# Cross-attention coefficients and a gelu table load later in the loop body, one more wait for GpSimd's subtract, and 60 transposes of the identity before the first expert block

## What is computed

```python
x = x + attn(layernorm(x))            # one head, q = W x/|x|, scores q (A q)^T / 16, softmax, times v, times |x|
x = x + xattn(layernorm(x), context)  # 4 heads of 64, mask, softmax over 1601 rows, @ Wo
# feed-forward
idx = argmax(softmax(x @ Wg + bg))
h   = gelu(x @ W1[idx] + b1[idx])     # 1024 wide
x   = x + h @ W2[idx] + b2[idx]
```

## Time and profile before

| | |
|---|---|
| median of 3 runs | 874.06 us (873.71 to 874.42) |
| the profiled execution's own time | 875.33 us |
| its span, first to last instruction | 873.6 us |
| mean granted TensorE clock | 0.945 of full speed |
| TensorE busy in matmuls | 767.2 us, 88% of the span |
| VectorE busy | 665.9 us, 76% |
| ScalarE busy | 461.4 us, 53% |
| GpSimd busy | 165.2 us, 19% |

### The profile page before, as it was taken

How to read it: one execution, slowest core, us unless ns; L and a number is a source line. 1 busy time by engine, 2 the same in 40 slices (tenths; PEclk the granted TensorE clock), 3 DMA queues, 4 the chain that set the end, 5 groups by cost and what they waited for, 6 DMA issues and landing times. The chain is left out here.

```text
span 873.6 us, 19805 instructions
## 1 busy us (share of the span) xinstructions
PE 767.2 (88%) x6136; PEld 692.5 (79%) x6137; DVE 665.9 (76%) x1608; ACT 461.4 (53%) x930; POOL 165.2 (19%) x254
## 2 busy tenths in 40 slices
PE   3879799989999898999989899998988753999996
PEld 2769689978888797988879788887987642889996
DVE  5974647888887888888888888888888744777773
ACT  2544536665565755656565565666656530444342
POOL 3100121130312303021130302203021111222221
PEclk9999989999999999999999999999999965999999
DMA  6242251321212132131322202132149292011110
GB/s 205 68 134 68 70 197 41 117 85 48 100 36 94 57 104 100 30 100 36 100 75 80 100 30 100 36 124 100 30 133 406 88 357 65 22 39 50 36 32 15
DMA packets 51142, 80.88 MB, mean 93 GB/s; under 512 B 4894, under 2 KB 29216, under 8 KB 50976
## 3 DMA queue, kind: packets, MB, share of 16 engines
q1 hardware_dynamic: 49232, 75.63, 25.9%
q0 software_dynamic: 1872, 4.76, 1.5%
HBM read 45.60 MB, written 35.18 MB: 92 GB/s over the span
## 5 line engine op out<-in xcount | busy, mean ns | idle before, releaser
L1126 ACT ACTIVATE ps_cross<-flip 128x512 f16<-128x512 f32 (+1 forms) x256 | 124.6, 514 | 113.5 <-PE flip L845 92.3
L1351 DVE TENSOR_TENSOR ps_cross<-flip,ps_cross 128x512 f16<-128x512 f32 (+1 forms) x256 | 143.6, 582 | 10.3 <-ACT ps_cross L1126 9.9
L845 PE MATMUL flip<-ident,exp_cross 128*128 128x128 f32 (+1 forms) x832 | 132.3, 282 | 8.5 <-DVE ps_cross L1351 5.1
L834 PE MATMUL scores<-keys_cross,qt 128*128 128x402 f32 x512 | 133.3, 385 | 4.3 <-DVE xneg L1511 2.3
L1312 ACT ACTIVATE exp_cross<-exp_cross,xneg 128x1024 f32<-128x1024 f32 (+1 forms) x128 | 122.7, 960 | 15.1 <-DVE xneg L1511 15.0
L856 PE MATMUL cross_out<-vals_cross,ps_cross 128*128 128x128 f16 (+1 forms) x832 | 105.3, 228 | 28.3 <-DVE ps_cross L1351 28.2
L856 PEld LDWEIGHTS cross_out<-vals_cross,ps_cross 128*128 128x128 f16 (+1 forms) x832 | 78.5, 104 | 51.9 <-DVE ps_cross L1351 36.5
L845 PEld LDWEIGHTS flip<-ident,exp_cross 128*128 128x128 f32 (+1 forms) x832 | 96.0, 143 | 16.3 <-DVE ps_cross L1351 6.6
L722 PE MATMUL scores<-keys_self,u_tile 128*128 128x512 f32 x384 | 102.5, 404 | 6.3 <-issue 4.6
L821 PE MATMUL flip<-vals_self,ps_self 128*128 128x256 f32 x768 | 104.0, 289 | 0.0
L858 PE MATMUL cross_out<-vals_cross,ps_cross 128*128 128x64 f16 (+1 forms) x832 | 98.2, 198 | 0.0
(11 more groups left out here) (197 smaller groups left out, 1240.8 us busy)
## 6 DMA issues: line engine op xcount, KB each, us to landing
rows_dram<-pads SPq DMA_DIRECT2D x17, 520.0 KB, 3.9
w_piece<-W SPq DMA_DIRECT2D x32, 256.0 KB, 2.9
w_dram<-w_high SPq DMA_DIRECT2D x32, 256.0 KB, 2.3
w_dram<-w_piece SPq DMA_DIRECT2D x32, 256.0 KB, 2.7
w1s<-w_dram SPq DMA_DIRECT2D x8, 1024.0 KB, 11.3
w2s<-w_dram SPq DMA_DIRECT2D x8, 1024.0 KB, 10.8
u_dram<-u_out SPq DMA_DIRECT2D x4, 1024.0 KB, 5.9
u_tile<-u_dram SPq DMA_DIRECT2D x16, 256.0 KB, 2.8
```

What stands on the lines that cost most here:

```text
L834: mm = pe.matmul(scores[:, n, 0:KB], qt[:, h, :], keys_cross[:, part, h, n * KB:(n + 1) * KB], start=(part == 0), stop=(part == 1))
L845: tr = pe.transpose(flip[0:rows, bank(use), n * P:(n + 1) * P], exp_cross[:, h % 2, m * P:m * P + rows], ident[:, :])
L1126: return act.activation(out, in_, ACT.Copy, **kw)
L1351: return dve.tensor_tensor(out, full, hi, ALU.subtract)
```

## The change

Four edits. GpSimd's subtract in body j waits for `self_max` of that body too. The three coefficient operations on VectorE move from behind `sneg` to behind `self_lo(1)`, ahead of `cross_max(0,1)`. The one-element gelu moves in body 17 from the front to behind `cross_hi(3,3)`. And TensorE gets 60 transposes of the identity, without a wait, between the last `rank` and the wait for `x2_ready`; they write into a bank of `scores` that nobody reads.

```diff
@@ gpsimd
                 pool.wait_ge(piece_hi, j + 1)
+                pool.wait_ge(self_max, j + 1)
                 pool.tensor_tensor(w_piece[:, :, :], w_piece[:, :, :].bitcast(F32), w_high[:, :, :].bitcast(F32),
                                    ALU.subtract).then_inc(piece_lo, 1)
@@ tensor
         run_pipeline(pe, body)
+
+        for n in range(60):
+            pe.transpose(scores[:, 3, 0:P], ident[:, :], ident[:, :])
         pe.wait_ge(x2_ready, T)
@@ scalar
             a, b, c = k < T, 1 <= k <= T, k >= 2
-            if k == T + 1:
-
-                act.activation(barrier[:, 1:2], ident[:, 0:1], ACT.Gelu).then_inc(gelu_table, 1)
             if c:
                 cross_hi(j, k, 2, 2)
...
             if c:
                 cross_hi(j, k, 3, 3)
+            if k == T + 1:
+
+                act.activation(barrier[:, 1:2], ident[:, 0:1], ACT.Gelu).then_inc(gelu_table, 1)
@@ vector
             if c:
-
-                dve.wait_ge(cross_exp_ready, 8 * (j - 1))
-                dve.tensor_tensor(xcoef[:, 2, :], xden[:, 0, :], xden[:, 1, :], ALU.add).then_inc(o_step, 1)
-                dve.wait_ge(o_step, 3 * (j - 1) - 2)
-                dve.reciprocal(xcoef[:, 0, :], xcoef[:, 2, :]).then_inc(o_step, 1)
-                dve.wait_ge(o_step, 3 * (j - 1) - 1)
-                dve.tensor_scalar(xcoef[:, 1, :], xcoef[:, 0, :], v_scale[:, 1:2], None, ALU.mult).then_inc(o_step, 1)
                 cross_lo(j, k, 3, 0)
                 cross_lo(j, k, 3, 1)
                 cross_lo(j, k, 3, 2)
             if b:
                 cross_max(j, k, 0, 0)
             if a:
                 self_lo(j, k, 0)
             if c:
                 cross_lo(j, k, 3, 3)
             if a:
                 self_lo(j, k, 1)
+            if c:
+                dve.wait_ge(cross_exp_ready, 8 * (j - 1))
+                dve.tensor_tensor(xcoef[:, 2, :], xden[:, 0, :], xden[:, 1, :], ALU.add).then_inc(o_step, 1)
+                ...
+                dve.tensor_scalar(xcoef[:, 1, :], xcoef[:, 0, :], v_scale[:, 1:2], None, ALU.mult).then_inc(o_step, 1)
             if b:
                 cross_max(j, k, 0, 1)
```

More of the change, by code:

```diff
@@ L1558, in body @@
                 self_lo(j, k, 1)
+            if c:
+                dve.wait_ge(cross_exp_ready, 8 * (j - 1))
+                dve.tensor_tensor(xcoef[:, 2, :], xden[:, 0, :], xden[:, 1, :], ALU.add).then_inc(o_step, 1)
+                dve.wait_ge(o_step, 3 * (j - 1) - 2)
+                dve.reciprocal(xcoef[:, 0, :], xcoef[:, 2, :]).then_inc(o_step, 1)
+                dve.wait_ge(o_step, 3 * (j - 1) - 1)
+                dve.tensor_scalar(xcoef[:, 1, :], xcoef[:, 0, :], v_scale[:, 1:2], None, ALU.mult).then_inc(o_step, 1)
             if b:
```

## The result

The changed kernel takes **829.77 us** in the median of 4 runs (826.53 to 830.76), against 873.88 for the kernel before (4 runs beside them, 871.21 to 874.42): a ratio of 0.9495, with a 95% interval of 0.9462 to 0.9527. The forecast was 827.5, with a range of 822 to 836. The profiled execution took 830.19 us, its span 828.4 against 873.6.

The account below looks back on a forecast made before the run. GpSimd's subtract holding VectorE's multiply was taken to pause TensorE and mostly slow its clock. Terms -41.95, -3.8, +0.1, +0.5, +0.3, -1.4, -0.3 sum to -46.55: 828.8 us profiled, 827.5 median, range 822 to 836.

Parts of the forecast that it names:

- The hold: After `sneg`, GpSimd's subtract holds VectorE's 128x4 coefficient multiply for 2.1 us, so `cross_lo(3,0)` is late and TensorE idles 2.08 us.
- A body of 34.1 us: Looped middle bodies fall to 34.1 us (ends 33.3 and 34.7); 12 bodies give -41.95 us (ends -51.5 and -34.8).
- the push: The moved coefficient operations delay `cross_max(0,1)` and `self_lo(2)` on VectorE, charged 0.1 us a body (ends 0 and 0.7).
- The clock: In the loop, TensorE's pause mostly brings the slow clock, worth 1.5 us a body; new bodies should have 1.00.
- Body 15 and 16: Body 15 loses its pause and slow stretch, -3.8 us; in body 16 the coefficients come behind the mask-bias wait, +0.5.
- Body 17: Coefficients stand ahead of the sum over `cross_out`, +0.3 us; the later gelu table load hides in ScalarE's idle time, -1.4.
- GpSimd's wait: The subtract's extra wait on `self_max` costs 0: already met in bodies 3 to 15, hidden in bodies 1 and 2.
- Transposes: 60 transposes behind the last `rank` bring the clock back before the first expert product: -0.3 us (ends -1.75 and +2.7).
- The rival with a chance of 0.32: The 60 transposes stay at the slow clock and hold `flip_x` by 2.7 us: 830.5 us; chance 0.32.
- The rival on the other side: Slower than before: the multiply meets GpSimd's subtract at its new place, TensorE pauses and loses its clock: about 877 us; chance 0.03.
- The sum: All terms over the whole kernel sum to -46.55 us: profiled execution 875.33 to 828.8 us, median 827.5.
- The start: Stretch up to `sneg` of body 3: body 2 gains nothing and pays the push, +0.1 us.

Follow-up runs that it names:

- the meeting at the new place: The changed kernel, but GpSimd's subtract waits for `self_lo(0)`, so it runs while VectorE reaches the moved coefficients: 851.15 us, ratio 0.9748.
- the load alone: The kernel before with only the one-element gelu (the table load) moved behind `cross_hi(3,3)` in body 17: one run, 872.82 us.

## Why the prediction was right, step by step

- **The hold.** Right, and shown: the multiply is at 0.229 us; with the coefficients left in place and the subtract moved behind them the gain is the same or better; with the subtract put back onto them half of the gain goes. The prediction had told apart by rows which operations pass (one input in PSUM) and which do not, and this held for `cross_lo` and `self_lo`. The Trainium skill, "SBUF — State Buffer", section "Who interferes with whom", has a rule of which I made no use: VectorE and GpSimd share a pair of SBUF ports; a VectorE operation with two SBUF inputs contends with a GpSimd operation that reads SBUF, and one in a two-port mode contends with GpSimd, where whoever issues first keeps the pair for the whole instruction. These traces agree: the add (two inputs in SBUF) was held for 1.6 us, the multiply for 2.1, each to the end of the subtract, and no operation with an input in PSUM. That the multiply, with one SBUF tensor and a column of factors, runs in a two-port mode is what the rule would need; no run shows its mode.
- **A body of 34.1 us.** Measured 34.23 in the middle and 34.00 at the end, 410.80 us for 12 against 409.2: the term is 40.35 and not 41.95, the one that was sized wrong by most. I had taken body 13, less its pause, plus 0.1 for the push. In the three kernels without the push (the coefficients at their old place, the subtract behind them) the 12 bodies take 408.82 to 409.47 us. So the push is worth 0.11 to 0.17 us a body, and the rest of the miss is that a body without it takes 34.07 to 34.12 and not 34.01. The prediction kept away from body 2's 33.3 because a looped body pays for its branch and for waits against registers. That such a body is longer is borne out (34.23 against 33.41 after the change, of which 0.44 is idle time of TensorE and 0.38 busy time); what in the loop costs it no run shows.
- **The clock.** Right: 1.00 over all 12 bodies. But the pause alone doesn't decide it: 2.05 to 2.44 us of pause lose it in 11 of the 12 looped bodies before the change and 2.13 us don't in body 13; the 1.65 us of the kernel with the meeting at the new place lose it in none of 12.
- **Body 15 and 16.** Forecast -3.8 and +0.5, so -3.3; measured -3.14 together. Body 16 is a poor place for terms of this size: its wait for the mask bias alone is between under 0.2 and 2.5 us in these kernels.
- **Body 17.** Forecast +0.3 and -1.4; measured -1.6 together. The kernel with the load alone has the same 19.93 us as the changed one, and the one with the coefficients alone 21.62 against the 21.53 before, so the coefficients cost about 0.1 us there and not 0.3: the sum over `cross_out` would wait for its matmuls anyway, and starts 0.14 us behind the last of them where it started 0.04 behind.
- **GpSimd's wait.** Zero was right for this kernel, but the reason was incomplete. I named only ScalarE as the one who might suffer. By itself the wait costs 1.6 us in body 2, since it moves the subtract onto the coefficients; only the other edit made it free.
- **Transposes.** Forecast: the clock back after 3.7 us, the last one 8.4 us behind the first, -0.3 in sum. Measured 3.9, 8.65 and -0.8, with a spread over the kernels that is as large as the effect. The rival with a chance of 0.32, that transposes stay slow, is false: the clock rose in their midst wherever they were tried (no 60 of them took the 12.8 us that slow ones need). Its price was 830.5; the 830.6 in the paragraph on the transposes is 0.1 too high for the same sum. The rule behind it (the Trainium skill, "TensorE: Matmul & The Clock Gate", Part 4) doesn't hold for these fp32 transposes, at 0.213 us each before the rise and 0.109 behind it; what that page measured is a bf16 transpose.
- **The rival on the other side** had the right mechanism and a wrong price. I gave 877 us for a multiply held at the new place, with the slow clock in every body. The run that does it took 851: there it is the add that is held, the pause is 1.65 us and not 2.1, and the clock stays. That GpSimd would not get there by itself was right: it is idle when the coefficients come.
- **The sum.** 828.8 was forecast for the profiled execution, and 830.19 measured. The loop is 1.6 us above its forecast, the start 0.5 and bodies 15 and 16 0.2; body 17 and the transposes are 0.5 each below. That these small terms mostly cancel is luck, and they are within what differs from kernel to kernel without an edit. The 1.27 us between execution and median of the kernel before were 0.42 here, which is the rest of the 2.3 us between 827.5 and 829.77.
- **The start**, +0.6, is for the most part no effect of the change: body 2 has the +0.1 of the forecast (33.41 against 33.30), and the other 0.5 us stand already at the `sneg` of body 1. This one, ahead of which only GpSimd's wait differs, starts between 120.35 and 124.46 us over the twelve kernels.

## What to carry to other kernels

When a tiny operation shows a median far above its minimum, look which other engine's instruction ends at the same moment. Here, where both had all their inputs in SBUF, it was enough to move either. Moving the one that nobody waits for was 1.1 to 2.0 us better over 12 bodies, too little for the times to tell. A wait that orders two engines is only worth what it keeps apart: check each body for what it brings together. And work that is to keep TensorE's clock up must reach up to the work that needs it: 60 transposes with 3.5 to 4.0 us of pauses behind them gave under a microsecond, 87 with pauses of 0.4 and 0.9 us gave 2.2.

## What the runs showed that was not expected

Transposes of fp32 alone, with no other matmul, bring TensorE's clock from 0.50 to 1.00: after 3.9 us in the changed kernel, after 3.2 and 4.4 in the ones with transposes alone and with 70 of them. The clock does not fall at once behind a pause: in the changed kernel it was still 1.00 when the product began behind pauses of 1.58 and 2.04 us, and fell some 1.5 us into it, when TensorE had been busy again. That is not how it always goes: in the kernel with the meeting at the new place, with pauses of 1.42 and 2.07 us behind the same 60 transposes, it fell in the second pause, 1.6 us ahead of the product, which then took 5.42 us. And GpSimd's mask bias, a 1.53 us operation, holds VectorE's add of 128x4 as the subtract holds the multiply: 0.35 us in nearly every body before the change (its duration was 146 ns at the shortest and 496 in the median), which the forecast hadn't seen since `cross_lo(3,0)` was late for a larger reason.
